# Layer 1 of a graph network: SyncE fetches three gathered columns in two rounds of three chunks

## The reference, cut to what matters

```python
h = x
msgs = x[src]
summed = jax.ops.segment_sum(msgs, dst, num_segments=num_nodes)
counts = jax.ops.segment_sum(jnp.ones((edge_index.shape[1],), x.dtype), dst, num_segments=num_nodes)
agg = summed / jnp.maximum(counts, 1.0)[:, None]
out = agg @ W_l.T + b_l
out = jax.nn.relu(out + x @ W_r.T)
return out + h
```

## Time and profile before

| what | value |
|---|---|
| median of three runs | 4535.75 us (4522.78 to 4539.2) |
| profiled execution | 4529.45 us, span of its instructions 4527.6 us |
| GpSimd busy | 3300.4 us, 73% of the span, 3493 instructions |
| VectorE busy | 2281.5 us, 50% |
| TensorE, ScalarE busy | 931.8 us, 785.6 us |
| layer 1's gathers, line 575 to `sb_big` from `x` | 1549 DMAs, from 2404 us to 4341 us of the span |

### The profile page before, as it was taken

How to read it: one execution, slowest core, us unless ns; L and a number is a source line. 1 busy time by engine, 2 the same in 40 slices (tenths; PEclk the granted TensorE clock), 3 DMA queues, 4 the chain that set the end, 5 groups by cost and what they waited for, 6 DMA issues and landing times. The chain is left out here.

```text
span 4527.6 us, 46280 instructions
## 1 busy us (share of the span) xinstructions
PE 931.8 (21%) x3091; PEld 613.9 (14%) x3091; DVE 2281.5 (50%) x9502; ACT 785.6 (17%) x1441; POOL 3300.4 (73%) x3493
## 2 busy tenths in 40 slices
PE   7301112111112000000293221122222221112027
PEld 7301101001001000000151110011111111001025
DVE  2107656666566666566473444344344344334348
ACT  2001101001001000000052222222222222222125
POOL 6677777777777777777565777777777777777755
PEclk6555555556556555555585555555555555555569
DMA  9803243333333322224284656666666666666769
GB/s 349 316 27 123 87 132 97 97 122 97 98 122 96 109 81 89 81 81 138 70 269 161 223 206 213 241 240 241 240 228 214 229 213 207 219 240 232 256 219 322
DMA packets 347584, 795.44 MB, mean 176 GB/s; under 512 B 94902, under 2 KB 235419, under 8 KB 317796
## 3 DMA queue, kind: packets, MB, share of 16 engines
q1 hardware_dynamic: 164706, 380.87, 23.6%
q0 software_dynamic: 137712, 276.64, 20.2%
q10 hardware_dynamic: 44818, 135.00, 7.7%
HBM read 420.40 MB, written 371.83 MB: 175 GB/s over the span
## 5 line engine op out<-in xcount | busy, mean ns | idle before, releaser
L575 POOL DMA_INDIRECT sb_big<-x,sb_idx x1549 | 1464.6, 946 | 502.8 <-issue 471.8
L575 POOL DMA_INDIRECT sb_big<-zu_rows,sb_idx x1531 | 1445.2, 944 | 478.4 <-issue 466.3
L1466 DVE SCALAR_TENSOR_TENSOR ps_V<-ps_V,sb_keepc,sb_big 128x256 f32<-128x256 f32 x1518 | 747.6, 493 | 132.7 <-ACT sb_big L1053 79.4
L1053 ACT COPY sb_big<-ps_V 128x1024 f32<-128x1024 f32 (+1 forms) x414 | 399.5, 966 | 1288.2 <-DVE ps_V L1466 1285.3
L762 PE MATMUL ps_T<-sb_ident,sb_xg 128*128 128x128 f32 x392 | 114.6, 390 | 2402.6 <-ACT sb_tileT L898 1225.0
L1466 DVE SCALAR_TENSOR_TENSOR ps_V<-ps_E,sb_keepc,sb_big 128x256 f32<-128x256 f32 x46 | 22.7, 492 | 1020.4 <-DMA sb_big<-x,sb_idx 981.0
L762 PEld LDWEIGHTS ps_T<-sb_ident,sb_xg 128*128 128x128 f32 x392 | 72.1, 201 | 2461.0 <-ACT sb_tileT L898 1236.2
L1272 DVE TENSOR_TENSOR_SCAN sb_big<-ps_E,sb_big 128x34 f32<-128x34 f32 x2944 | 355.3, 203 | 1.6
L1220 DVE TENSOR_TENSOR_SCAN ps_V<-ps_V,sb_big 128x34 f32<-128x34 f32 x2944 | 354.6, 206 | 0.0
L1229 DVE TENSOR_TENSOR sb_big<-ps_V,sb_big 128x2176 f32<-128x2176 f32 x46 | 111.4, 2421 | 351.3 <-DMA sb_big<-zu_rows,sb_idx 351.3
L575 POOL DMA_INDIRECT sb_hn<-rows,sb_nidx x196 | 189.5, 967 | 75.3 <-issue 53.6
(11 more groups left out here) (240 smaller groups left out, 1845.7 us busy)
## 6 DMA issues: line engine op xcount, KB each, us to landing
rows<-sb_big SPq DMA_DIRECT2D x46, 3072.0 KB, 10.7
rows<-sb_big SPq DMA_DIRECT2D x46, 1280.0 KB, 13.8
rows<-sb_big ACTq DMA_DIRECT2D x46, 1224.0 KB
z_at_start<-sb_big ACTq DMA_DIRECT2D x46, 1088.0 KB, 8.7
sb_big<-z_at_start SPq DMA_DIRECT2D x46, 1088.0 KB, 5.2
sb_zx<-zu_rows SPq DMA_DIRECT2D x2816, 0.2 KB
sb_big<-x SPq DMA_DIRECT2D x1920, 1.0 KB
sb_xg<-in_x_dram SPq DMA_DIRECT2D x36, 768.0 KB, 6.2
```

Source lines behind the costliest of these rows:

```text
L575: pool.indirect_dma_start(to, None, table, bass.IndirectOffsetOnAxis(ap=index.bitcast(U32), axis=0), **more).then_inc(done, 16)
L1053: act.copy(slot1[s][:, cols, :], V0[:, first_word:first_word + width].rearrange("p (c f) -> p c f", f=D)).then_inc(col_copied, 1)
L1466: dve.scalar_tensor_tensor(out=sums_at(j), in0=before, scalar=keepc[:, j:j + 1], in1=slot1[s][:, j, :], op0=ALU.mult, op1=ALU.add).then_in ...
```

## The change

A third column is taken from GpSimd and given to SyncE: in every second round (the odd ones, for the first 14 rounds) the last column of slot 2. It concerns seven chunks: 5, 11, 17, 23, 29, 35 and 41.

- `row_bytes` gets a third table with those seven columns' addresses, `stage` a third row. One more small VectorE instruction makes the table, and both SyncE and ScalarE wait for `rows_scaled` to be 4 and not 3.
- SyncE's rounds are written in pairs (`rows1_rounds`). In an even round it also stages the third table's column, and after the store of slot 2 it calls `fetch_row2`: this waits for that store to land and then issues 128 DMAs for the chunk of the following odd round. After it comes the next round's store of slot 0.
- GpSimd issues 33 gathers and not 34 for slot 2 in odd rounds. Its loop and VectorE's now go over pairs of rounds (7), and the last four chunks stand behind the loops.
- VectorE's wait for slot 2's gathers counts the missing one, and in odd rounds it waits for the fetched rows before column 33 of slot 2.

The semaphores `stage_loaded[0]` and `row_fetched[0]` of layer 0 are counted on for the new fetches.

```diff
+            def fetch_row2(i, pair):
+                sp.wait_ge(stage_loaded[0], 16 * (NCH // 2) + 16 * pair)
+                sp.sem_inc(gate, 1)
+                sp.wait_ge(r_stored[2], 32 * (i + 1))
+                sp.sem_inc(gate, 1)
+                fetch_rows(2, slot1[2][:, C - 1, :], x1, D)
+
+            def rows1_rounds(pair, last=False):
+                for odd in range(2):
+                    i = 2 * pair + odd
+                    store_rows1(i, 0)
+                    bg_store(1, i)
+                    if not (last and odd == 1):
+                        bg_load(1, i + 1)
+                    stage_rows(1, i + 1)
+                    if odd == 0:
+                        stage_rows(2, pair)
+                    store_rows1(i, 1)
+                    fetch_row1(i + 1)
+                    store_rows1(i, 2)
+                    if odd == 0:
+                        fetch_row2(i, pair)
...
-            def gather_rows1(i, s):
+            def gather_rows1(i, s, odd):
                 pool.wait_ge(idx1_ready[s], i + 1)
                 wait(pool, r_stored[s], 32 * i)
                 pool.sem_inc(gate, 1)
-                for j in range(C - 1 if s == 1 else C):
+                for j in range(C - 1 if s == 1 or (s == 2 and odd) else C):
                     gather(slot1[s][:, j, :], x1, idx[s][:, j:j + 1], r_gathered[int(j >= CA)][s])
...
-                        dve.wait_ge(r_gathered[1][s], 16 * (C - CA - (s == 1)) * (i + 1))
+                        if s == 2:
+                            dve.wait_ge(r_gathered[1][s], 16 * ((1 + odd) * (C - CA) - odd) + 16 * (2 * (C - CA) - 1) * pair)
+                        else:
+                            dve.wait_ge(r_gathered[1][s], 16 * (C - CA - (s == 1)) * (i + 1))
                     if j == C - 1 and s == 1:
                         dve.wait_ge(row_fetched[1], 16 * P * (i + 1))
+                    if j == C - 1 and s == 2 and odd:
+                        dve.wait_ge(row_fetched[0], 16 * P * (NCH // 2) + 16 * P * pair)
```

More of the change, by code:

```diff
@@ L82, in gnn_kernel @@
     NX = 4
-    assert FP * FQ == NF and FQ * FW <= C * F and CA % GC == 0 and NGC % 2 == 1 and C % GC == 2 and NG * GB == NB and NG % NX == 2 and NCH % 4 == 2 and NCH % S1 == 1 and NCH % 2 == 0 and NG < NCH // S1 and 0 < ELAST <= COLS and NF * FW == E
+    assert FP * FQ == NF and FQ * FW <= C * F and CA % GC == 0 and NGC % 2 == 1 and C % GC == 2 and NG * GB == NB and NG % NX == 2 and NCH % 4 == 2 and NCH % S1 == 1 and NCH % 2 == 0 and S1 * NG <= NCH < S1 * NG + 2 * S1 and 0 < ELAST <= COLS and NF * FW == E
     assert E <= EP and D == 2 * P
@@ L210, in gnn_kernel @@
         idx = [sb(f"idx{s}", [P, C], I32) for s in range(S1)]
-        row_bytes = [sb(f"row_bytes{k}", [P, n], I32) for k, n in ((0, NCH // 2), (1, NCH // S1))]
-        stage = sb("stage", [1, 2, P], I32)
+        row_bytes = [sb(f"row_bytes{k}", [P, n], I32) for k, n in ((0, NCH // 2), (1, NCH // S1), (2, NG // 2))]
+        stage = sb("stage", [1, 3, P], I32)
         zx = sb("zx", [P, F])
@@ L426, in stage_rows @@
                     sp.dma_start(stage[0:1, layer, :], row_bytes[layer][:, bass.ds(i, 1)]
-                                 ).then_inc(stage_loaded[layer], 16)
+                                 ).then_inc(stage_loaded[layer % 2], 16)
             def fetch_rows(layer, to, table, width):
@@ L435, in fetch_rows @@
                         sp.dma_start(to[p0 + k:p0 + k + 1, :].bitcast(U8), flat[:, bass.ds(at_byte, 4 * width)]
-                                     ).then_inc(row_fetched[layer], 16)
+                                     ).then_inc(row_fetched[layer % 2], 16)
             def load_zd(i):
@@ L452, in _ @@
             bg_load(0, 0)
-            sp.wait_ge(rows_scaled, 3)
+            sp.wait_ge(rows_scaled, 4)
             fetch_zx(0)
@@ L526, in _ @@
             fetch_row1(0)
-            with sp.Fori(0, NG - 1) as i:
-                rows1_round(i)
-            rows1_round(NG - 1, last_background=True)
+            with sp.Fori(0, NG // 2 - 1) as pair:
+                rows1_rounds(pair)
+            rows1_rounds(NG // 2 - 1, last=True)
             for k in range(S1 * NG, NCH - 2):
@@ L647, in gather_rows1 @@
                 pool.sem_inc(gate, 1)
-                for j in range(C - 1 if s == 1 else C):
+                for j in range(C - 1 if s == 1 or (s == 2 and odd) else C):
                     gather(slot1[s][:, j, :], x1, idx[s][:, j:j + 1], r_gathered[int(j >= CA)][s])
-            rounds(pool, NCH // S1, lambda i: [gather_rows1(i, s) for s in range(S1)])
-            for s in range(NCH % S1):
-                gather_rows1(NCH // S1, s)
+            rounds(pool, NG // 2, lambda pair: [gather_rows1(2 * pair + odd, s, odd) for odd in range(2) for s in range(S1)])
+            for c in range(S1 * NG, NCH):
+                gather_rows1(c // S1, c % S1, 0)
             for s in range(S1):
@@ L966, in weights_of_edges @@
                             stage_rows(pair + 1)
-            act.wait_ge(rows_scaled, 3)
+            act.wait_ge(rows_scaled, 4)
             stage_rows(0)
@@ L1189, in _ @@
                                              ).then_inc(w_dve, 1)
-            for k, step, width in ((0, 2, F), (1, S1, D)):
-                last_cols = src_i[:, 0:NCH // step * step * C].rearrange("p (i c) -> p i c", c=step * C)[:, :, 2 * C - 1]
+            for k, step, at_chunk, n, width in ((0, 2, 1, NCH // 2, F), (1, S1, 1, NCH // S1, D), (2, 2 * S1, S1 + 2, NG // 2, D)):
+                last_cols = src_i[:, 0:n * step * C].rearrange("p (i c) -> p i c", c=step * C)[:, :, at_chunk * C + C - 1]
                 dve.tensor_scalar(row_bytes[k][:, :], last_cols, float(4 * width), None, ALU.mult
@@ L1444, in _, with sum_rows @@
                 dve.tensor_copy(idx[s][:, :], src_i[:, s * C:(s + 1) * C]).then_inc(idx1_ready[s], 1)
-            def sum_rows(i, s):
+            def sum_rows(i, s, pair, odd):
                 c = S1 * i + s
@@ L1471, in sum_rows @@
                 dve.tensor_copy(car, sums_at(C - 1)).then_inc(car1_saved, 1)
-            rounds(dve, NCH // S1, lambda i: [sum_rows(i, s) for s in range(S1)])
-            for s in range(NCH % S1):
-                sum_rows(NCH // S1, s)
+            rounds(dve, NG // 2, lambda pair: [sum_rows(2 * pair + odd, s, pair, odd) for odd in range(2) for s in range(S1)])
+            for c in range(S1 * NG, NCH):
+                sum_rows(c // S1, c % S1, NG // 2, 0)
             mend(dve.memset(got[:, :], 0.0))
```

## The result

The changed kernel takes 4725.1 us (4723.2 to 4726.9, four runs), the kernel before 4537.5 us beside it. The ratio is 1.0445 with a 95% interval of 1.0417 to 1.0474: slower by 4.2 to 4.7%. The profiled execution took 4723.2 us against 4529.4 before, 193.7 us more. The prediction was 4778 us, range 4694 to 4862.

What follows compares the result with a forecast made beforehand. GpSimd's gathers bound the kernel before; the change makes SyncE the bound at 289 us per pair against 251.4. Six such pairs less 1485.4 us add 248.6 to 4529.45, giving 4778 us, range 4694 to 4862.

Steps and rivals of the forecast that it cites:

- the gain is 8.8 us: Layer 1, GpSimd: seven gathers removed at 1.25 us each, 8.8 us or 0.19% of the time.
- 66 us idle in a pair: SyncE before the change: waits of 15, 4, 8 and about 6 us, 33 us per round, 66 per pair.
- 78.8 more: SyncE's added work per pair of rounds: L of 15.7 us plus F of 63.1 us.
- the rival: The hidden fetch: SyncE's pair stays under 251.4 us and GpSimd does not wait; 4521 us, chance 5%.
- First pair: Round 1's slot 0 store is issued at 2657.8 us, 70 us late; GpSimd's first stall is some 16 us.
- F: SyncE's fetch, from a store's landing to the next store behind the fetch: 63.1 us, 61.5 of it 128 issues.
- L: SyncE's store, from issuing two parts together to the landing of the second: 15.7 us.
- The bursts: SyncE's stores and background loads up to slot 1's landing: 53.4 us in even rounds, 37.8 in odd.
- 7 for the gathers that stand still: Saving per pair in store bursts because stalled GpSimd gathers don't share bandwidth: up to 9 us, taken as 7.
- the cap that I had given: Upper limit on the bursts' saving per pair while GpSimd stands idle: up to 9 us.
- P: SyncE's time for a pair of rounds in layer 1: 289 us, against 251.4 for GpSimd.
- The hidden fetch: SyncE's pair stays under 251.4 us, so stores are late but GpSimd does not wait: 4521 us, chance 5%.

Runs made afterwards that it cites:

- without the column: Changed kernel with GpSimd's 33 gathers but no new fetch, so the column is left out; run twice: stretch 1927.3 and 1927.7 us, time 4530.8 and 4513.8 us.
- rows 64, 96 and 128: Changed kernel with the new fetch issuing 64 or 96 rows instead of its 128: 4578.5 and 4655.6 us, against 4725.1 us with 128.
- quarter_rows: Changed kernel, but each of the new fetch's 128 row DMAs moves 256 bytes and not 1 KB: 4733.5 us.
- pairs_only: Changed kernel keeping the loops over pairs, but the new column goes back to GpSimd (34 gathers, no third staging or new fetch): 4530.5 us.
- act_stores: Changed kernel, but slot 2's stores of the first 42 chunks are issued by ScalarE behind its copies, not by SyncE: 4697.1 us.
- fetch_later: Changed kernel, but the new fetch stands in the odd round behind slot 0's store, the background and the staging: 4732.2 us.

## Why the prediction was right, point by point

- **GpSimd sets the pace before, and the gain is 8.8 us.** Right for the stretch, 9 us without the column; in the time it is too small to be told from none.
- **SyncE has 66 us idle in a pair and gets 78.8 more, so it leads.** Right, though 66 was too much. The waits of the earlier trace rows are 360.7 us in 14 rounds, some 52 in a pair. The rest is the 8 us per round between slot 2's store and slot 0's, which I took for a wait: most of it is the turn of SyncE's loop (below). The error was on the side of the rival, and the truth makes the case against it stronger. The rows 64, 96 and 128 give 259, 271 and 283 us per pair, all above 251.4.
- **First pair.** The store of slot 0 in round 1 was to come at 2657.8 us, 253.4 after the first gather. It came at 2645.61, 253.9 after it, and the first stall was 15.5 us where some 16 were forecast.
- **F = 63.1 and L = 15.7.** Measured 62.8, 62.7 and 63.0, and 15.3 us.
- **The bursts.** This is the mis-sized term. They were put at 53.4 and 37.8 less 7 for the gathers that stand still, 84.2 in all. Measured are 46.9 and 31.9, 78.8. The two together, without the 7, were 91.2, so they were 12.4 us too long where I took off 7. The 64 and 96 rows tell how much of it comes with the stalls: 7 us of burst for 25 us of stall, which for all 31 us makes an estimate of 9, the cap that I had given. By that estimate the sums of 53.4 and 37.8 were themselves 3 or 4 us too large; in which part is open.
- **The time.** P = 289 against 283.2. From the first late store to that of round 13 (1.2 us ahead of the row of line 416, at 4343.2) were 1697.6 us where 6 x 289 = 1734 were forecast, 36 us less. The end, from there to the last gather's end, took 191.4 us and not 197.5, 6 us less. And this execution began layer 1 at 2391.7 us and not at 2404.4, 13 us less, which is no effect of the change. 4778 - 36 - 6 - 13 = 4723, the profiled execution's time.
- **The hidden fetch** fell at the point where it was said to be decided. `quarter_rows` shows 61.5 us of SyncE for 128 rows of 256 bytes, as for rows of 1 KB. The Trainium skill ("DMA: Bandwidth & Descriptors", "Issuing engines are not separate DMA queues") says that starting a DMA usually takes little time beside the DMA itself. Read as "a fetch costs SyncE little", that does not hold here, with 0.48 us of SyncE per row; how long such a row's own transfer takes, no view shows.
- **What the profile would show.** Stalls of 215 us at the starts of slots 0 and 2, where near 250 were forecast; two fetches in even rounds; three waits for its own stores per pair; waits for ScalarE's copies all but gone. So SyncE leads alone, and no chain through VectorE.

One thing was not seen as what it is and did little harm. In the kernel after, SyncE is done with slot 2's store at 3309.45 and issues slot 0's at 3317.24, though that chunk's copy ended at 3278.4:

```profile
3277.35 1.02 ACT L1066 COPY sb_big<-ps_V 128x1024 f32<-128x1024 f32 x1
```

There the loop turns. In the last pair, which stands behind the loop, the same step takes 0.2 us (4156.92 to 4157.14). The burst of the last pair lasts no less, as it is the queue's bytes that last. `pairs_only` has half the loop turns of the kernel before: there the step takes 7.1 to 7.3 us where the loop turns and 3.0 to 5.2 us, a wait for copies, where it doesn't, and the time is the same. No run took the loop away altogether.

## What to carry to other kernels

A small DMA costs its issuer time per DMA, not per byte: handing one gather of GpSimd (1.25 us, 128 rows) to an engine that issues row by row costs that engine 61 us, so the receiving engine's whole round must be summed, waits for its own stores included, and compared with the round of the engine that leads. An idle share is not a budget where the idle time lies between stores whose bytes have to drain anyway: sum the time of the bytes and the time of the issues, since an engine that waits for landings before it issues has them one after the other. And when one engine's lateness makes another stall, the bursts beside the stall can get shorter and give back part of the loss (here 7 us of burst for 25 us of stall); leave room for it.

## What the runs showed of the hardware

- Row DMAs from SyncE mostly start 0.40 us apart for 256 bytes as for 1 KB (`quarter_rows` and the changed kernel), and 1.66 us apart where 16 addresses are loaded in between.
- While large stores from ScalarE's queue drain, those rows start 1.2 us apart (nine in 10.8 us, `act_stores`).
- At the turn of its long loop SyncE lost 7.2 to 8.4 us in the changed kernel, where a slot's store had just been issued, and 2.9 to 3.4 us in `act_stores`, where SyncE had issued rows before it; where no loop turns the step takes 0.2 us. What the time goes into was not tested.
- The profile files part of the waits for a store under "issue": single waits of 14, 18.5 and, in `fetch_later`, 32.7 us. In this kernel an "issue" entry whose longest wait is far above its mean is a semaphore wait.
